# Five shared batches ahead of the experts instead of four, the first one's up steps moved into attention, expert weights loaded into their final place, and the loop over pairs written out

## The chip, the cores and the metric

The kernel runs on one core of a Trainium2 chip. The metric is the time of one execution on the device, in microseconds (us). A core has TensorE (PE, matrix products), VectorE (DVE), ScalarE (ACT) and GpSimd (POOL), a SyncE (SP) that issues DMAs, and 16 DMA engines; each engine runs its own instructions in order, and they wait for one another by semaphores.

## The reference, cut to what matters

One transformer layer in fp32 on x of 8 batches x 512 tokens x 256 values.

```python
x = x + attention(layernorm(x))        # 16 heads of 16, causal, W_Q, W_K, W_V, W_O 256x256
n = layernorm(x)
# FFN of n, 4096 tokens
shared = silu(n @ shared_w_gate.T) * (n @ shared_w_up.T) @ shared_w_down.T    # 704 hidden values
shared = shared * sigmoid(n @ shared_gate_w.T)
probs = softmax(n @ gate_w.T)          # 16 experts
rw, sel = top_k(probs, 2); rw = rw / rw.sum(-1)
for each token and each of its 2 experts e:
    g, u = split(n @ w_gate_up[e]); out += rw * ((silu(g) * u) @ w_down[e])   # 128 hidden values
x = x + out + shared
```

## The kernel before, in words

Products that have to be exact are made of three: each fp32 operand is split into a high part (rounded, by a copy on ACT) and a low part (what is left, by a subtraction on DVE), and `exact_product` issues hi x hi, hi x lo and lo x hi (lines 177, 178, 179 of the profile).

The program has two blocks one after the other, with a barrier of all engines between them.

**Block 1, `build_attention`.** Every engine walks one hand-written list of steps, `TURN`, once per batch, each entry with an offset of batch: S are scores and exps, max the row maxima, PV the product with V, oT/oTT transposes of its result, O the output projection, x2T and L the transposed xn2 and the router's logits, R the top 8, W the split of the shared weights. The eight PSUM banks are taken in the order of the steps (`Schedule`); a step waits until the step eight banks earlier has been emptied. The last turn (it = 8) has only what is left of batch 7. In its end DVE normalises x1 to xn2 itself (L580), SP stores xn2 (L371) and x1 (L376), and PE makes the last logits (L807).

**Block 2, `build_ffn`.** Four stages:
- *First half*, batches 0 to 3 (`FIRST = 4`) of the shared FFN. `shared` on PE: six up steps (12 products of 128x512 each, 6 in the last, which holds 64 gate and 64 up rows), the transposes of the next batch (L1423), then the down product (72 products of 128x256). ACT does silu (L1120) and the high part of h (L1125), DVE the product (L1299), the low part (L1302), and at the batch's end adds gate x result to x1 (L1317). Beside batch 0 DVE does the routing (L1220 to L1254: counts, prefix sums, slots), one part behind each step, then the weights (L1212 to L1216) and `experts_of_tiles` (L1259 to L1267). Once the slots are known, POOL scatters the 4096 rows of xn2 twice to the experts' rows in HBM (L1091, 64 indirect DMAs). Beside batches 1 to 3 the 16 experts' weights come one by one through two staging buffers (L1003) and are split (L1136, L1339).
- *Pairs*: 80 tiles of 128 rows, as 40 pairs, each tile of one expert: load (L1012), transpose x (L1480), gate and up, silu and product, transpose h (L1497), down, result (L1158), store (L1016). `fours_loop` runs four pairs per turn: the first and last four are written out, the 32 pairs between run in a hardware loop with a register. PE reads the experts' numbers from SBUF at the head and in the middle of a turn (`experts_of`).
- *Second half*, batches 4 to 7 of the shared FFN. Beside them POOL gathers each token's two rows (L1103, 64 indirect DMAs), and DVE adds them with their weights (L1323) to the stored results of the batches 0 to 6, some tiles behind each step (`TILES_BESIDE`).
- The last four tiles' rows and the last batch's result are added at the very end and stored in two parts.

SP's list holds the loads of xn2 and x1 for each batch, the rows for the scatter, the experts and the stores, in one order. x1 of a batch is loaded only when the stored result of the one before has left its buffer, and rows for the scatter when the rows two batches earlier are scattered.

Of the kernel before, what the change touches and what calls it, by code (L numbers as in the profile page):

```python
# [5 lines left out]
P = 128  # L6
B, S, D = 8, 512, 256
# [43 lines left out]
for g in range(GROUPS):  # L51
# [10 lines left out]
    ("max", 0, 1, 1), ("max", 0, 1, 2), ("oTT", -1, 0), ("oTT", -1, 1), ("K", 1, 1), ("max", 0, 1, 3), ("S", 0, 0, 0, 0),  # L62
# [12 lines left out]
def steps_of_turn(it):  # L75

    steps = []
    for kind, offset, *rest in TURN:
        if kind == "W":
# [10 lines left out]
EMPTIED_BY = {"xT": "dve", "Q": "dve", "K": "dve", "max": "dve", "mT": "act", "V": "act", "oT": "dve", "oTT": "dve",  # L90
              "O": "dve", "x2T": "act", "L": "dve"}
BANKS_OF = {"S": HALVES, "PV": 1}
SPLIT_STEPS = ("xT", "Q", "K", "oTT")


class Schedule:
# [29 lines left out]
    def freed(self, kind, which, n=0):  # L126

        if kind == "S":
            b, u, g, p = which
            return "exp", HALVES * (PAIRS * (GROUPS * (UNITS * b + u) + g) + p) + n + 1  # L130
        if kind == "PV":
            return "copy", UNITS * GROUPS * which[0] + which[1] + 1
# [1468 lines left out]
```

## Time and profile before

| | |
|---|---|
| three runs | 805.0, 805.0 and 809.97 us, median 805.0 |
| profiled execution | 800.1 us, its span 798.4 us |
| mean granted TensorE clock | 0.966 |
| busy in the span | PE 711.2 us (89%), DVE 524.7, ACT 401.5, POOL 326.8 |
| block 2 begins | 444.05 us |
| first pair's product | 570.62 us |
| second half's first product | 694.37 us |

The span is the time from the first to the last recorded work; 1.7 us lie around it. A busy PE is not PE at its peak. The granted clock of 1.00 is 2.4 GHz, 0.50 is 1.2 GHz.

### The profile page before, as it was taken

To read this page: it belongs to the slowest core of one execution; us is meant where nothing else is said; L and a number is where in the kernel's file an instruction comes from. 1 tells how busy PE (TensorE), PEld (TensorE's weight loads), DVE (VectorE), ACT (ScalarE), POOL (GpSimd) and SP (SyncE) were. 2 spreads that over 40 slices of the span, in tenths; PEclk is the share of its full clock that TensorE was granted. 3 is DMA by queue.
4 is the path that set the end of the run, shared out by engine and by line. 5 is a ranking of instruction groups with operands and counts; after the bars stand their busy time and mean duration, and the time that the engine had idled before them with its cause. 6 is when DMAs were issued, how large, how long until landed. Compare 5 with 4: busy or idle time off the path is not lost. (4 is left out here: it accounts for less than half of the span.)

```text
span 798.4 us, 17094 instructions
## 1 busy us (share of the span) xinstructions
PE 711.2 (89%) x5970; PEld 560.7 (70%) x5971; DVE 524.7 (66%) x1158; ACT 401.5 (50%) x777; POOL 326.8 (41%) x678
## 2 busy tenths in 40 slices
PE   1489999999999999999874879999699999999997
PEld 1456576676767667676643678887599989888886
DVE  6287787888878787887814494465445444466667
ACT  3116657565765656676671223344266565533232
POOL 5203536272552627354571127577100000077771
PEclk9889999999999999999998798999799999999999
DMA  5578667575876757577041218777554554478763
GB/s 158 204 244 292 212 240 260 175 258 185 290 265 206 261 193 241 189 264 232 21 155 35 98 53 282 264 236 259 171 186 154 186 169 151 133 229 279 242 211 115
DMA packets 102503, 159.72 MB, mean 200 GB/s; under 512 B 7712, under 2 KB 78368, under 8 KB 98208
## 3 DMA queue, kind: packets, MB, share of 16 engines
q1 hardware_dynamic: 96288, 141.99, 53.3%
q0 software_dynamic: 6144, 16.79, 6.3%
q8 instruction: 44, 0.72, 0.4%
q14 instruction: 27, 0.22, 0.1%
HBM read 86.66 MB, written 71.83 MB: 199 GB/s over the span
## 5 line engine op out<-in xcount | busy, mean ns | idle before, releaser
L615 DVE TENSOR_REDUCE neg_max<-ps_w 128x1 f32<-128x512 f32 (+3 forms) x352 | 202.5, 632 | 43.5 <-PE ps_w L720 43.5
L552 ACT ACTIVATE probs<-ps_w 128x512 f32<-128x512 f32 x320 | 165.2, 617 | 9.9 <-PE ps_w L736 9.8
L401 POOL TENSOR_TENSOR pool_scratch<-minus_half 1x1 f32<-1x1 f32 x190 | 35.0, 184 | 237.0 <-ACT probs L552 201.1
L1103 POOL DMA_INDIRECT ex<-yg_dram,slots x64 | 65.1, 1017 | 153.9 <-DMA yg_dram<-y 134.7
L433 POOL TENSOR_SCALAR_AFFINE_SELECT probs<-probs 128x256 f32<-128x256 f32 (+1 forms) x224 | 94.1, 431 | 0.0
L1091 POOL DMA_INDIRECT xg_dram<-srow,slots x64 | 65.5, 1023 | 51.8 <-DVE slots L1254 26.6
L177 PE MATMUL ps_f<-stacks 128*128 128x512 f32 x176 | 72.7, 413 | 9.6 <-DVE xT_lo_f L1272 6.8
L1120 ACT ACTIVATE silu<-ps_f 128x512 f32<-128x512 f32 (+1 forms) x48 | 28.5, 594 | 103.7 <-PE ps_f L179 103.7
L747 PE MATMUL ps_w<-probs,v_aug 128*32 128x512 f32 (+3 forms) x1024 | 77.1, 442 | 3.8 <-POOL probs L433 3.8
L178 PE MATMUL ps_f<-xT_lo_f,stacks 128*128 128x512 f32 x176 | 70.8, 403 | 0.0
L179 PE MATMUL ps_f<-stacks 128*128 128x512 f32 x176 | 70.8, 402 | 0.0
L1299 DVE TENSOR_TENSOR h<-ps_f,silu 128x512 f32<-128x512 f32 (+1 forms) x48 | 33.1, 690 | 46.7 <-ACT silu L1120 44.7
L747 PEld LDWEIGHTS ps_w<-probs,v_aug 128*32 128x32 f32 x1024 | 30.8, 111 | 44.7 <-issue 34.2
L560 ACT ACTIVATE o_raw<-ps_w 128x512 f32<-128x512 f32 x32 | 19.4, 606 | 76.3 <-PE ps_w L747 76.3
L177 PE MATMUL ps_f<-stacks,h_hi 128*128 128x256 f32 (+1 forms) x192 | 55.0, 286 | 1.8 <-DVE h_lo L1302 1.8
L177 PE MATMUL ps_f<-ex,stacks 128*128 x160 | 48.4, 302 | 5.8 <-issue 4.3
L179 PE MATMUL ps_f<-stacks,h_lo 128*128 128x256 f32 (+1 forms) x192 | 53.4, 278 | 0.0
L178 PE MATMUL ps_f<-w_lo,h_hi 128*128 128x256 f32 (+1 forms) x192 | 53.4, 278 | 0.0
L720 PE MATMUL ps_w<-mask_rows,ident_rows 64*128 64x128 bf16 (+2 forms) x704 | 53.2, 229 | 0.0
L712 PE MATMUL ps_w<-stacks 64*128 64x256 f32 (+3 forms) x256 | 41.4, 376 | 10.8 <-DMA stacks<-qk_dram 10.2
L1353 DVE TENSOR_TENSOR h<-ps_f,silu 128x256 f32<-128x256 f32 x40 | 17.0, 424 | 48.6 <-ACT silu L1148 48.6
L177 PEld LDWEIGHTS ps_f<-stacks 128*128 128x128 f32 x176 | 34.1, 194 | 20.1 <-DVE xT_lo_f L1272 6.4
(170 smaller groups left out, 1792.5 us busy)
## 6 DMA issues: line engine op xcount, KB each, us to landing
qk_dram<-projected SPq DMA_DIRECT2D x96, 256.0 KB, 5.6
stacks<-qk_dram SPq DMA_DIRECT2D x16, 1024.0 KB, 7.3
xg_dram<-zeros SPq DMA_DIRECT2D x20, 512.0 KB, 10.3
srow<-xg_dram SPq DMA_DIRECT2D x40, 256.0 KB, 2.8
q_st<-qk_dram SPq DMA_DIRECT2D x8, 1024.0 KB, 5.0
k_st<-qk_dram SPq DMA_DIRECT2D x8, 1024.0 KB, 8.3
projected<-experts SPq DMA_DIRECT2D x16, 384.0 KB, 4.9
yg_dram<-projected SPq DMA_DIRECT2D x20, 256.0 KB, 2.2
```

The lines of the kernel that those rows point to most:

```text
L177: pe.matmul(out, s_hi, m_hi, start=start, stop=False)
L178: pe.matmul(out, s_hi, m_lo, start=False, stop=False)
L179: return pe.matmul(out, s_lo, m_hi, start=False, stop=stop)
L401: ticks = Ticks(pool, pool_ticks, lambda: pool.tensor_tensor(out=pool_scratch[:, 0:1], in0=minus_half[0:1, 0:1], in1=minus_half[0:1, 0:1], ...
L433: masked = pool.affine_select(out=diagonal, in_=diagonal, compare_op=ALU.is_ge, fill=0.0, base=0, pattern=[[0, number], [1, P]], channel_m ...
L552: act.activation(probs[:, g, p * PAIR + half * BANK:p * PAIR + (half + 1) * BANK], ps_w[:, plan.bank(kind, which, half), :], ACT.Exp).then ...
L615: dve.tensor_reduce(out=neg_max[u][:, qt, first:first + len(heads)], in_=bank[:, 0:len(heads) * width].rearrange("p (h n) -> p h n", h=len ...
L712: pe.matmul(outs[half][:, i * width:(i + 1) * width], q_st[u][b % 2][rows, slot, qt * P:(qt + 1) * P], k_st[u][b % 2][rows, slot, 0:width] ...
L720: made = pe.matmul(blocks, ident_rows[rows, part, :], mask_rows[rows, part, first:P].unsqueeze(1).to_broadcast([ROWS, len(heads), P - first]),
L747: made = pe.matmul(out[hh * STRIP:(hh + 1) * STRIP, kt * P:S], v_aug[b % 2][:, kt, group * GH + hh, :], probs[:, g, pair * PAIR + col:pair ...
L1091: pool.indirect_dma_start(out=xg_rows, out_offset=bass.IndirectOffsetOnAxis(ap=slots[:, c, n:n + 1], axis=0), in_=srow[:, b % 2, t, :], in ...
L1103: pool.indirect_dma_start(out=back[:, m, c, :], out_offset=None, in_=yg_rows, in_offset=bass.IndirectOffsetOnAxis(ap=slots[:, c, m:m + 1], ...
```

## The change

1. `FIRST = 5`: batches 0 to 4 of the shared FFN run ahead of the experts, 5 to 7 behind them. `EXPERTS_FROM` gives four experts to split to each of the batches 1 to 4; `TILES_BESIDE` spreads the 28 tiles over three batches.
2. Batch 0's transposes (`fT`) and up steps (`U` 0 to 6; step j also splits h of j-1) are steps of attention's last turn. Their operands and results get memory that both blocks share. In block 2, batch 0 has its down product alone; its result is added by DVE behind the second step of batch 1. Batch 1's transposes come first in block 2, and SP loads its xn2 at the end of block 1.
3. DVE does the whole routing in one go in batch 0's place, `experts_of_tiles` behind the third step of batch 1. The ranks go to banks 4 and 5.
4. The experts' weights come in four loads of four experts, straight to where their low parts will stand; ACT makes the high part from there and DVE the low part in place. The loads are issued at the start of block 2.
5. The rows for the scatter are loaded beside batches 1 to 3 (`SCATTERED_BESIDE`).
6. The loop over pairs becomes one slot per pair, written out 41 times, on all four engines; the experts' numbers are read at each even pair.

```diff
 TURN = [
...
+    ("S", -1, 1, 1, 1), ("fT", 8, 0), ("fT", 8, 1), ("max", 0, 0, 6), ("R", -2), ("S", -1, 1, 1, 2),
...
+    ("S", -1, 1, 1, 4), ("PV", -1, 2), ("U", 8, 0),
...
+    ("PV", -1, 3), ("oT", -1, 2), ("mT", 0, 0), ("oT", -1, 3), ("U", 8, 1),
...
+    ("oTT", -1, 0), ("oTT", -1, 1), ("U", 8, 2),
...
+    ("O", -1, 1), ("moments_x1", -1), ("U", 8, 3), ("U", 8, 4),
...
+    ("x2T", -1, 0), ("x2T", -1, 1), ("U", 8, 5),
...
+    ("L", -1, 1), ("U", 8, 6),
...
 ]
...
         sp.wait_ge(first_in, 16)
+        sp.wait_ge(work_ready, plan.upto("ready", "fT", DK - 1))
+        sp.dma_start(xn_f, xn2_v[1]).then_inc(first_in, 16)
+        sp.wait_ge(first_in, 32)
...
@@ ACT, a step of block 1 @@
+            elif kind == "fT":
+                act.activation(xf_hi[:, which, :], bank, ACT.Copy).then_inc(hi_done, 1)
+            elif kind == "U":
+                if which < FT:
+                    act.wait_ge(up_made, which + 1)
+                    if which >= 2:
+                        act.wait_ge(h_made, which - 1)
+                    act.activation(silu[0:filled(which), which % 2, :], ps_w[0:filled(which), plan.bank(kind, which), :], ACT.Silu).then_inc(silu_made, 1)
+                if which > 0:
+                    act.wait_ge(h_made, which)
+                    part = filled(which - 1)
+                    act.activation(h_hi[0:part, which - 1, :], h[0:part, (which - 1) % 2, :], ACT.Copy).then_inc(h_hi_made, 1)
...
@@ PE, a step of block 1 @@
+        def shared_up(j):
+            if j == 0:
+                pe.wait_ge(freed["dve"], plan.freed("fT", DK - 1)[1])
+                pe.wait_ge(shared_lo, 4)
+            for i in range(banks_of("U", j)):
+                out, col = bank_for("U", j, i), (2 * j + i) * P
+                for k in range(DK):
+                    at = slice(k * 2 * FF + col, k * 2 * FF + col + P)
+                    made = exact_product(pe, out, (up_parts[0][:, at], up_parts[1][:, at]), (xf_hi[:, k, :], xT_lo[:, k, :]),
+                                         start=k == 0, stop=k == DK - 1)
+            made.then_inc(up_made, 1)
...
-FIRST = 4
+FIRST = 5
-EXPERTS_FROM = [0, 0, 5, 10, 16]
-TILES_BESIDE = {4: (0, 1, 1, 1, 1, 1, 2), 5: (1, 1, 1, 1, 1, 1, 1), 6: (1, 1, 1, 1, 1, 1, 1), 7: (1, 1, 1, 1, 1, 1, 1)}
+EXPERTS_FROM = [0, 0, 4, 8, 12, 16]
+LOADS = 4
+PER_LOAD = E // LOADS
+TILES_BESIDE = {5: (0, 1, 1, 2, 1, 2, 1), 6: (1, 2, 1, 2, 1, 2, 1), 7: (1, 2, 1, 2, 1, 2, 1)}
+SCATTERED_BESIDE = {0: (), 1: (2, 3, 4), 2: (5, 6), 3: (7,), 4: ()}
...
@@ SP, block 2 @@
             load_x1(b)
-            for e in range(EXPERTS_FROM[b], EXPERTS_FROM[b + 1]):
-                if e >= 2:
-                    sp.wait_ge(w_split, e - 1)
-                sp.dma_start(stage[:, e % 2, :], experts[e]).then_inc(stage_in[e % 2], 16)
-                if e % 2 and e // 2 < B - 2:
-                    rows_of(e // 2 + 2)
+            for ahead in SCATTERED_BESIDE[b]:
+                rows_of(ahead)
             sp.wait_ge(y_done, TB * (b + 1))
...
         for b in range(2):
             rows_of(b)
+        for n in range(LOADS):
+            some = slice(n * PER_LOAD, (n + 1) * PER_LOAD)
+            sp.dma_start(ex[:, some, 1, :].bitcast(f32), experts[some].rearrange("e p n -> p e n")).then_inc(experts_in[n], 16)
...
@@ DVE, block 2 @@
         def shared(b, more, beside):
+            if b == 0:
+                for j in range(FT + 1):
+                    routing(j)
+                weights()
+                return
             for j in range(FT + 1):
...
                 if j >= 1:
                     beside(j - 1)
-                if b == 0:
-                    routing(j)
-            if b == 0:
-                weights()
-                experts_of_tiles()
+                if b == 1 and j == 1:
+                    add_shared(0)
+                if b == 1 and j == 2:
+                    experts_of_tiles()
...
@@ PE, block 2 @@
         def shared(b, more):
+            if b:
+                up(b)
+            if b and more:
+                transpose_xn(b + 1)
+            down(b)
...
+        def slot(n):
+            if is_pair(n - 1):
+                transpose_h(n - 1)
+            if n >= 0:
+                transpose_x(n + 2) if is_pair(n + 2) else transpose_xn(FIRST, [n + 2 - TILE_PAIRS]) if n + 2 < TILE_PAIRS + DK else None
+            if is_pair(n + 1):
+                gate_and_up(n + 1)
+            if is_pair(n - 1):
+                project_down(n - 1)
...
+        def start(b):
+            transpose_xn(b + 1)
+            ranks()
...
+        for n in range(-1, TILE_PAIRS + 1):
+            slot(n)
```

## Rows read from the trace of the kernel before

**Rows 1.** Busy time by window, the stage ahead of the experts; the last figure is GB/s
```profile
444.00:564.00 120.00, 107.14 (x586) 90.72 (x586) 73.48 (x126) 44.51 (x74) 66.85 (x70) 0.94 0.60 202
```
**Rows 2.** The chain that ended last, where the pairs begin: start, us, what
```profile
564.35 3.42 DMA srow<-xg_dram
...
570.62 0.57 PE ps_f L177
```
**Rows 3.** The source line of the scatters
```profile
L1091 POOL DMA_INDIRECT xg_dram<-srow,slots x64: 957/963/1614, 472.2 to 561.8; - x64
```
**Rows 4.** Timeline of DVE, routing beside batch 0
```profile
453.24 0.68 DVE L1220 COPY projected<-ps_f 128x512 f32<-128x512 f32 x1
...
471.67 0.20 DVE L1254 CAST slots<-projected 128x64 int32<-128x64 f32 x1
...
472.87 0.82 DVE L1259 TENSOR_TENSOR y<-projected 128x640 f32<-128x640 f32 x1
...
477.51 1.29 DVE L1272 TENSOR_TENSOR xT_lo_f<-ps_f,stacks 128x512 fp32r<-128x512 f32 x2
```
**Rows 5.** The chain, two batches of the second half: their transposes
```profile
709.91 0.88 PE ps_f L1423 x8
...
734.94 0.87 PE ps_f L1423 x8
```
**Rows 6.** The source line of the gathers; the second row is of its last nine
```profile
L1103 POOL DMA_INDIRECT ex<-yg_dram,slots x64: 945/949/1395, 697.5 to 780.8; - x64
...
DMA to landing us min/median/max: 2.7/3.5/5.5
```
**Rows 7.** Timeline of PE, one turn of the loop over pairs
```profile
633.04 0.38 PE L177 MATMUL ps_f<-ex,stacks 128*128 x1 [0.60 <-issue]
...
641.99 0.44 PE L1497 MATMUL ps_f<-ident,h 128*128 128x128 f32 x2
...
644.43 0.28 PE L179 MATMUL ps_f<-ex,h_lo 128*128 x1
645.33 0.38 PE L177 MATMUL ps_f<-ex,stacks 128*128 x1 [0.62 <-issue]
```
**Rows 8.** Timeline of PE, attention's tail; in brackets the idle time before
```profile
418.47 2.36 PE L747 MATMUL ps_w<-probs,v_aug 128*32 128x512 f32 x32 [1.98 <-POOL probs L433]
...
423.07 1.09 PE L683 MATMUL ps_w<-ident,o_tok 128*128 128x128 f32 x8 [0.81 <-DVE o_tok L624]
425.74 0.39 PE L177 MATMUL ps_w<-w_hi,oT_hi 128*128 128x256 f32 x1 [1.57 <-DVE oT_lo L595]
...
436.12 1.97 PE L683 MATMUL ps_w<-ident,xn 128*128 128x128 f32 x8 [7.25 <-DVE xn L580]
```
**Rows 9.** Timeline of PE, first up products of batch 1
```profile
478.86 0.79 PE L177 MATMUL ps_f<-stacks 128*128 128x512 f32 x1 [4.41 <-DVE xT_lo_f L1272]
...
484.57 0.52 PE L178 MATMUL ps_f<-xT_lo_f,stacks 128*128 128x512 f32 x1
484.92 0.39 PE L179 MATMUL ps_f<-stacks 128*128 128x512 f32 x1
485.15 0.40 PE L177 MATMUL ps_f<-stacks 128*128 128x512 f32 x1
```
**Rows 10.** Timeline of ACT, the last exps
```profile
407.58 9.90 ACT L552 ACTIVATE probs<-ps_w 128x512 f32<-128x512 f32 x20
```
**Rows 11.** DMA issues from 426 to 450: KB each, us to landing
```profile
srow<-xn_dram SPq DMA_DIRECT2D x2, 512.0 KB, 4.3
...
x_dram<-x SPq DMA_DIRECT2D x1, 512.0 KB, 5.5
```
**Rows 12.** Busy time by window, behind the border: granted clock, DMA share, GB/s at the end
```profile
446.00:447.00 1.00, 0.03 (x1) 0.00 (x0) 0.84 (x2) 0.91 (x2) 0.00 (x0) 0.50 1.06 372
```
**Rows 13.** Timelines of PE and DVE, where the second half begins and ends
```profile
694.37 0.47 PE L177 MATMUL ps_f<-stacks 128*128 128x512 f32 x1 [0.97 <-DVE xT_lo_f L1272]
...
794.08 1.66 DVE L1317 SCALAR_TENSOR_TENSOR projected<-ps_f,gate,projected 128x256 f32<-128x256 f32 x4
```

More of the change, by code:

```diff
@@ L104, in __init__ @@
         assert len(self.place) == len(self.steps)
-        self.banked = [(*step, n) for step in self.steps for n in range(BANKS_OF.get(step[0], step[0] in EMPTIED_BY))]
+        self.banked = [(*step, n) for step in self.steps for n in range(banks_of(*step))]
         self.banked_place = {step: n for n, step in enumerate(self.banked)}
@@ L763, in step @@
                 transposed(kind, which, xn)
+            elif kind == "fT":
+                out = bank_for(kind, which)
+                pe.wait_ge(first_in, 16)
+                for t in range(TB):
+                    made = pe.transpose(out[:, t * P:(t + 1) * P], xn_f[:, t, which * P:(which + 1) * P], ident[:, :])
+                made.then_inc(work_ready, 1)
+            elif kind == "U":
+                if which < FT:
+                    shared_up(which)
             elif kind in ("Q", "K"):
@@ L863, in ffn_views, with shared_views, filled, build_ffn @@
             rows.rearrange("p (t d) -> p t d", t=TB), others.rearrange("p (t d) -> p t d", t=TB))
-def build_ffn(nc, ctx, stacks, projected, w_lo, logits_all, top, index, slots, experts_of_four, weight, gate, x1_dram, xn2_dram, xg_dram, yg_dram, y1_dram,
+def shared_views(stacks, rows_held, heads_held):
+    xT_hi = stacks[:, 2 * UP_COLS + DOWN_COLS:2 * UP_COLS + DOWN_COLS + DK * S].rearrange("p (k t) -> p k t", k=DK)
+    silu, h = (rows_held[:, n].rearrange("p (two t) -> p two t", two=2) for n in range(2))
+    h_hi, h_lo = (heads_held[:, n * FT * S:(n + 1) * FT * S].rearrange("p (j t) -> p j t", j=FT) for n in range(2))
+    return xT_hi, silu, h, h_hi, h_lo
+def filled(j):
+    return P if j < FT - 1 else FF_LAST
+def build_ffn(nc, ctx, stacks, projected, w_lo, x_lower, rows_held, heads_held, logits_all, top, index, slots, experts_of_four, weight, gate, x1_dram, xn2_dram, xg_dram, yg_dram, y1_dram,
               ident, experts, out):
@@ L1178, in tiles @@
         def tiles():
             act.wait_ge(x1_left, 16 * FIRST)
[L1180 to L1186 removed]
+            for q in range(2):
+                split_x(q)
+            slots_of_loop(slot)
+        def start(b):
+            act.wait_ge(args_ready, 2)
+            act.activation(exps[:, :, :], args[:, :, :], ACT.Exp).then_inc(exps_ready, 1)
+            split_xT(b + 1)
@@ L1188, in _ @@
+        two_halves(start, first_half, tiles, shared)
     @block.vector
@@ L1313, in shared @@
             beside(FT)
-            dve.wait_ge(x1_in, 16 * (b + 1))
-            for t in range(TB):
-                dve.wait_ge(down_ready, b * 2 + (t // 2 + 1))
-                dve.scalar_tensor_tensor(out=x1[:, t, :], in0=ps[:, 6 + t // 2, (t % 2) * D:(t % 2 + 1) * D],
-                                         scalar=gate[:, bass.ds(b * TB + t, 1)], in1=x1[:, t, :], op0=ALU.mult, op1=ALU.add).then_inc(y_done, 1)
+            add_shared(b)
         def add_rows(c, m, done):
@@ L1444, in shared, with down @@
                 last.then_inc(up_ready, 1)
-                if b == 0 and j == 0:
-                    ranks()
-            if b == 0:
-                pe.wait_ge(counts_left, 1)
-                pe.wait_ge(routing_steps, RANK_READ)
-            if more:
-                transpose_xn(b + 1)
+        def down(b):
             pe.wait_ge(y_done, b * TB)
```

341 lines of the change are left out of this document (164 added, 177 removed), and 19 rows, old and new, of the table TURN.

## Prediction

> **What bounds the kernel now.** I cut the span by stage (busy time by window, then the timelines) and asked in each what ends last, since TensorE (PE) is at nine tenths or more almost everywhere and the page's totals don't tell. Attention lasts to 444.05, the four shared batches ahead of the experts to 561.7, the 40 pairs from 570.62 to 693.2, the four batches behind them to 794, and the stores to 798.4. Ahead of the experts PE is busy for 107 of 120 us [rows 1], and the chain of waits shows that it isn't what ends last: behind the last of 64 scatters on GpSimd (POOL) come its landing, a load, a transpose and a split [rows 2]. The scatters run from 472.2, when the slots are known, to 561.8 [rows 3, 4]. Four batches want 100 us of PE there (25.0 each, by the undisturbed ones [rows 5]) and get 117. Behind the experts it is PE: 694.37 + 4 x 25 = 794, while the 64 gathers start their last at 780.8 [rows 6]. The pairs run at 12.29 us per four, with an idle of 0.6 at the loop's head [rows 7]. In attention's tail PE is free for much of the time, but a single chain (exp, mask, P V, transposes, output projection, norm) runs through it, and PE is one of its links [rows 8].
>
> I write A for the start of the second block (444.05 before) and set up its new value first.
>
> **Attention's tail.** It gains two transposes of xn2 and 66 products of 512 columns, 0.23 us apart [rows 9]: 15.3 us of PE, with six silus and eight copies on ScalarE (ACT) and 14 operations on VectorE (DVE).
> - The two copies of the transposes stand among 20 exps, which run without a gap at 9.90/20 = 0.50 each [rows 10]: 1.0 on the chain.
> - U(8,0), 12 products or 2.8 us, stands between the last two P V. The last one was at 418.47 [rows 8]; now the one ahead of it ends at 417.5, U(8,0) at 420.3: 1.8 later with the exps' 1.0.
> - U(8,1) stands between the o transposes and those of o_tok. PE was idle there for 0.81 to 1.0 [rows 8]: 1.8 more.
> - U(8,2) fills the 1.57 idle ahead of the output projection [rows 8] and pushes it by 1.2; its operations and those of U(8,1) are queued on DVE around the lowering of oT, 0.1 more. The last x1, its norm and xn2 come at 436.06 + 4.9 = 440.9.
> - U(8,3) and U(8,4), 5.6 us, fit into PE's 7.25 idle [rows 8] and cost nothing; U(8,5), U(8,6) and the logits end before what follows. If that cover were short, every us would go onto the chain.
> - The load of silu's table falls into ACT's wait for U(8,0).
> - SP now loads xn2 of batch 1 inside this block, behind its waits for both stores. The x1 store, SP's second issue behind xn2 (0.4 later), lands 5.5 after it [rows 11], so 5.9 behind xn2; issue and landing of the new load are 0.4 + 4.3 [rows 11], the barrier 0.2. The block ends 10.8 behind xn2, where it was 8.0.
> A is 440.9 + 10.8 = 451.7: **7.7 later**. For the bounds: 4 if the fills fit better, 11 if the product steps queue up on DVE.
>
> **Ahead of the experts.** Batch 0 has only its down product left, five batches in place of four.
> - DVE does the choices first; the ranks can run at A+3.6, so the down product of batch 0 starts at A+4.9. PE is again at 0.50 of its clock (1.2 GHz) after the idle at the border, as behind the border before [rows 12]; 8.9 (25.0 less 15.3 and the 0.9 of the transposes [rows 5]) and some 1.1 for the clock: A+14.9.
> - Routing no longer alternates with batch 0's steps. Its operations from places to slots add up to 9.8 (18 of them, before spread over 453.24 to 471.87 [rows 4]); from A+5.2 the slots are ready at A+15.0, before at A+27.8. Even with the 89.6 that the scatters took with their waits [rows 3], the rows are complete at A+108. This was the bound and is none now.
> - Batch 1's steps queue on DVE behind routing. Its second step is followed by the add of batch 0's result, which waits for x1. That load is issued at A+15.1, behind two row loads and four expert loads, 7.3 MB in all. At the 372 GB/s of a busy stretch [rows 12], and 260 once the scatters' 100 (128 KB per 1.27 us) go beside it, it lands at A+26; unhindered, with the 4.3 of [rows 11], at A+20. I take 26: the x1 store in the tail, issued behind a single other one, already took 5.5 and not 4.3 [rows 11]. Then come the adds, one step, and experts_of_tiles, 4.65 us [rows 4], ahead of the next step. PE waits twice, 2.0 and 4.1 us. The second is as long as the 4.4 before 478.86, behind which the products were 0.43 apart up to 484.57, and 0.23 from 484.92 [rows 9]: 5.7 us at half clock, or 2.9 lost. Batch 1 costs 25.0 + 9.0 (bounds 4 and 13): A+48.9.
> - Two batches of 25.05 and one of 24.15 (no transposes behind it) end at A+123.2. The experts' split from their final place removes 16 loads of 384 KB and the waits for the staging buffers; what is left, a copy on ACT and a subtraction on DVE for each expert, four of them in a batch's 25 us, hides under PE; without that cover it would be near 1 us each on DVE.
> - Then SP has the store of the last y1 (1.2 + 0.4) ahead of the first pair's load, and from the issue of that load to the first pair's product it takes 6.3 [rows 2], with 0.6 more for the store in the queue: 8.5. First product at **A+131.7**; before at A+126.6. That is 5.1 later.
>
> The Trainium skill (DMA: Bandwidth & Descriptors, "Queues, rings and completion order") states that each DMA engine consumes the descriptors of one ring in order, and takes turns between rings at packet boundaries. By it x1 comes behind the experts as I set it; at A+20 the batch would cost 2.2 less. No row of before shows the order, since no load stood behind that much.
>
> **The pairs.** The order written out is: transpose h, transpose x, gate and up, down. At the old loop's head the first product starts 0.90 behind the last one, where 0.12 is usual, and two transposes of h come 0.17 late in the body: 12.29 less 0.78 and 0.17 is 11.34 per four [rows 7]. Over nine heads that gives 8.6. At the end nothing stands between the last transposes of h and the down products: two waits for a copy and a subtraction, by an estimate 0.8 each, 1.6 given back. **7 less**; 9 if those waits are covered, nothing if each of the 20 reads of the experts' numbers costs 0.4, out of the 0.6 that the head shows.
>
> **Behind the experts.** Three batches end 75 us behind the pairs, so PE no longer ends last. The gathers keep their pace, 83.3 from first to last start, and start 4.3 behind the last pair, whose products end just ahead of 693.4 [rows 6, 13]. The last lands 3.2 on (landings are 2.7 to 5.5 [rows 6]); one first add and four second ones (2.1), 1.7 for the adds of the last batch and 2.7 for its store [rows 13] follow: 697.5 + 83.3 + 3.2 + 2.1 + 0.1 + 1.7 + 2.7 = 790.6 on the old scale, against 798.4: **7.7 less** with rounding. A whole batch of 25 us less gives only this, because the gathers come next. Bounds 6 and 8.5.
>
> **The sum.** 7.7 + 5.1 - 7 - 7.7 = -1.9. The profiled execution had a span of 798.4 in a time of 800.1, 1.7 around it, which stays: 798.2. The median of the runs shown is 805.0, 4.9 above the profiled one; the same difference taken from it gives **803.1**. The 15 us of up steps are not removed from PE, and the batch that they belong to is moved from a stage where PE was the bound to one where it was not, but becomes it.
>
> **Rivals.** (1) *The clock stays up and the slots run dry of waits.* The waits of 2.0 and 4.1 come from estimates. Were the second shorter, and the clock stayed up, 2.9 and the 1.1 of batch 0's down part go, and the pairs give 9 and not 7: 803.1 - 6 = **797**. For it: the new up steps keep PE at work closer to the border; against it: behind idles of 4.4 and 7.25 the clock was at 0.50 [rows 8, 9, 12]. (2) *The written-out pairs give nothing*: the head's 0.6 is the number read and not the branch. For it: the releaser is "issue" and nothing else is seen there; against it: the same read stands in the middle of the body, where no idle shows. 803.1 + 7 = **810**. (3) *The expert loads are slow* (the other side). They are 6.3 MB in four issues with x1 behind them, and batch 0's add blocks DVE, and so batch 1's steps and PE. At 372 GB/s it costs 2; the mean of the stage is 202 [rows 1]. At that, 7.3 MB are there at A+38, x1 at A+41, 15 us later: 803.1 + 15 = **818**. It turns the sign at a mean of about 310 GB/s and gives over 1% slower under about 235. Against it: three loads in a row ran at 372 [rows 12]. (4) *The tail isn't filled but pushed*, each of the first five product steps with its whole 2.8 on the chain: 4 more, **807**.
>
> **How the numbers follow.** Forecast 0.48 (its own range 799 to 808), (1) 0.22, (2) 0.11, (3) 0.10, (4) 0.09. One per cent (8 us) is about what a measurement of this kernel can tell from no change, since its three runs differ by 5. Faster by more than that: (1) with most of its chance and the low end of the forecast, 0.24. Slower: (3) and a share of (2), 0.13. Within it: 0.63. The range of 794 to 812 leaves out the greater part of (3) and a corner of (1) and (2).
>
> **What would show it.** Right: second block at about 452; first scatter some 15 us behind it; PE idle for 2 and 4 us in batch 1's up steps, with the clock at 0.50 behind them; no idle of POOL that PE waits for ahead of the experts, and PE the last there; 11.3 per four pairs; DVE waiting for gathers in the last 20 us. Wrong: x1 landed well before batch 1's second product; gaps of 0.3 and more at each second pair; PE, not the gathers, last at the end.

## The result, and the profile after

| | before | after |
|---|---|---|
| median, first comparison | 805.44 us (805.0 to 809.97, 4 runs) | 796.01 us (794.73 to 797.4, 4 runs) |
| profiled execution, its span | 800.1, 798.4 us | 796.59, 794.8 us |
| median, timed again in a later comparison | 803.63 us (11 runs) | 795.66 us (6 runs) |

The ratio to the kernel before is 0.9868, 95% interval 0.9833 to 0.9902, and when timed again 0.9902 (0.9879 to 0.9925). The kernel is about 1% faster, 8 to 9 us. The forecast was 803, inside a range of 794 to 812. The time lies in the range, but 7 us under the forecast and outside the likeliest case's own range of 799 to 808.

The rows below are of the changed kernel. First busy time by window, ahead of the experts, in the columns of [rows 1]:
```profile
452.00:573.00 121.00, 113.88 (x658) 100.30 (x658) 75.08 (x128) 45.71 (x75) 68.85 (x70) 0.95 0.60 209
```
PE idles for 7 us in a stretch where it idled for 13 [rows 1]: it has become the last. The chain that ended last (start, us, what) says the same. What leads to the first pair is the last result of the fifth batch and its store, and not a step of POOL as in the chain of [rows 2]:
```profile
572.47 1.67 DVE projected L1366 x4
574.15 0.36 SPq L1080
574.61 3.60 DMA srow<-xg_dram
...
581.06 0.58 PE ps_f L186
```
The source line of the scatters, against [rows 3]: they begin 4.7 us earlier, counted from the start of the execution, although the second block begins 8.4 later, and the last one begins 27 us ahead of the first pair's product.
```profile
L1165 POOL DMA_INDIRECT xg_dram<-srow,slots x64: 957/963/1691, 467.5 to 554.3; - x64
```
The timeline of DVE: the slots are ready 14.5 us behind the start of the block at 452.48 (before 27.6 [rows 4]), and batch 0's result waits for x1 (idle time and releaser in brackets).
```profile
466.99 0.20 DVE L1325 CAST slots<-projected 128x64 int32<-128x64 f32 x1
...
477.50 1.66 DVE L1366 SCALAR_TENSOR_TENSOR projected<-ps_f,gate,projected 128x256 f32<-128x256 f32 x4 [1.56 <-DMA projected<-x_dram]
```
The timeline of PE, in three places: the tail of attention [rows 8], the two waits in batch 1's up steps [rows 9], and the pairs [rows 7].
```profile
415.67 4.05 PE L789 MATMUL ps_w<-probs,v_aug 128*32 128x512 f32 x32 [0.62 <-DVE x_lower L621]
...
422.60 2.36 PE L789 MATMUL ps_w<-probs,v_aug 128*32 128x512 f32 x32
...
442.94 1.09 PE L725 MATMUL ps_w<-ident,xn 128*128 128x128 f32 x8 [1.81 <-DVE xn L606]
...
452.48 1.94 PE L1491 MATMUL ps_f<-ident,projected 128*128 128x128 f32 x8 [5.34 <-PEq L1632]
...
479.81 0.50 PE L186 MATMUL ps_f<-stacks 128*128 128x512 f32 x1 [1.32 <-DVE rows_held L1383]
...
486.34 0.50 PE L186 MATMUL ps_f<-stacks 128*128 128x512 f32 x1 [3.51 <-DVE rows_held L1383]
...
601.43 0.36 PE L186 MATMUL ps_f<-ex,stacks 128*128 x1
...
604.23 0.36 PE L186 MATMUL ps_f<-ex,stacks 128*128 x1
...
694.92 0.38 PE L186 MATMUL ps_f<-ex,heads_held 128*128 x1 [0.85 <-DVE heads_held L1437]
...
697.41 0.38 PE L186 MATMUL ps_f<-ex,heads_held 128*128 x1 [1.29 <-DVE heads_held L1437]
```
The 7.25 us in which PE waited for xn [rows 8] are down to 1.81: the up steps found idle time to fill there. From pair to pair it is 2.80 us without a gap, 11.2 per four, where the loop took 12.29 [rows 7]. Busy time by window, the third figure from the end of a row being the granted clock:
```profile
450.00:460.00 10.00, 5.71 (x24) 5.00 (x25) 6.34 (x12) 3.89 (x5) 1.50 (x7) 0.50 0.76 259
480.00:490.00 10.00, 6.49 (x27) 5.18 (x27) 9.70 (x18) 4.23 (x7) 6.76 (x7) 0.87 0.93 306
490.00:500.00 10.00, 10.00 (x76) 9.60 (x75) 4.43 (x9) 1.59 (x3) 7.84 (x8) 0.96 0.44 149
775.00:795.00 20.00, 4.54 (x37) 4.21 (x35) 8.95 (x20) 0.00 (x0) 9.04 (x9) 0.65 0.46 144
```
The last row shows PE at work for 4.54 of the last 20 us: behind the pairs it has become the gathers that end last. Their source line, against [rows 6], and the last adds on DVE, against [rows 13]:
```profile
L1177 POOL DMA_INDIRECT ex<-yg_dram,slots x64: 942/949/1457, 702.5 to 785.6; - x64
...
DMA to landing us min/median/max: 2.7/3.9/7.1
```
```profile
788.42 2.07 DVE L1402 SCALAR_TENSOR_TENSOR projected<-ex,weight,projected 128x256 f32<-128x256 f32 x5 [2.06 <-DMA ex<-yg_dram,slots]
790.53 1.66 DVE L1366 SCALAR_TENSOR_TENSOR projected<-ps_f,gate,projected 128x256 f32<-128x256 f32 x4
```

### The profile page after: what moved, and what is told of

Same layout as the page of the kernel before. It is cut to its first block and busy times, and to the rows that moved or that the text cites. A ratio compares the mean times of both kernels' runs of the same rounds, so it can differ in the third digit from the quotient of the medians.

```text
span 794.8 us, 16690 instructions
## 1 busy us (share of the span) xinstructions
PE 708.8 (89%) x5970; PEld 563.3 (71%) x5970; DVE 528.6 (67%) x1158; ACT 400.6 (50%) x779; POOL 328.1 (41%) x678
## 5 line engine op out<-in xcount | busy, mean ns | idle before, releaser
L1165 POOL DMA_INDIRECT xg_dram<-srow,slots x64 | 67.4, 1053 | 33.9 <-issue 18.9
L1196 ACT ACTIVATE rows_held<-ps_f 128x512 f32<-128x512 f32 (+1 forms) x42 | 25.0, 596 | 108.8 <-PE ps_f L188 108.8
L789 PE MATMUL ps_w<-probs,v_aug 128*32 128x512 f32 (+3 forms) x1024 | 78.9, 451 | 0.9 <-DVE x_lower L621 0.6
L186 PE MATMUL ps_f<-stacks 128*128 128x512 f32 x154 | 62.0, 403 | 9.4 <-DVE rows_held L1383 5.1
L188 PE MATMUL ps_f<-stacks 128*128 128x512 f32 x154 | 61.2, 398 | 0.0
L187 PE MATMUL ps_f<-x_lower,stacks 128*128 128x512 f32 x154 | 61.1, 397 | 0.0
L1383 DVE TENSOR_TENSOR rows_held<-ps_f,rows_held 128x512 f32<-128x512 f32 (+1 forms) x42 | 29.0, 691 | 43.1 <-ACT rows_held L1196 42.8
L186 PE MATMUL ps_f<-stacks,heads_held 128*128 128x256 f32 (+1 forms) x192 | 56.8, 296 | 0.0
L187 PE MATMUL ps_f<-w_lo,heads_held 128*128 128x256 f32 (+1 forms) x192 | 55.0, 287 | 0.0
L188 PE MATMUL ps_f<-stacks,heads_held 128*128 128x256 f32 (+1 forms) x192 | 54.8, 286 | 0.0
L186 PE MATMUL ps_f<-ex,stacks 128*128 x160 | 49.3, 308 | 0.8 <-DVE x_lower L1425 0.8
L187 PE MATMUL ps_f<-ex,stacks 128*128 x160 | 45.9, 287 | 0.0
L188 PE MATMUL ps_f<-ex,x_lower 128*128 x160 | 45.8, 287 | 0.0
## 6 DMA issues: line engine op xcount, KB each, us to landing
ex<-experts SPq DMA_DIRECT2D x4, 1536.0 KB, 14.7
```

The costliest lines, as they stand in the source:

```text
L186: pe.matmul(out, s_hi, m_hi, start=start, stop=False)
L187: pe.matmul(out, s_hi, m_lo, start=False, stop=False)
L188: return pe.matmul(out, s_lo, m_hi, start=False, stop=stop)
L789: made = pe.matmul(out[hh * STRIP:(hh + 1) * STRIP, kt * P:S], v_aug[b % 2][:, kt, group * GH + hh, :], probs[:, g, pair * PAIR + col:pair ...
L1165: pool.indirect_dma_start(out=xg_rows, out_offset=bass.IndirectOffsetOnAxis(ap=slots[:, c, n:n + 1], axis=0), in_=srow[:, b % 2, t, :], in ...
```

## Experiments

Twelve runs were made in three comparisons, each beside the kernel before. In all of them the same four points were read: A, the start of the second block (its first transposes), the first transposes of the pairs, the first gather, and the end of the span. What lies between them adds up to the span, but for rounding, in us:

| profiled execution | A | A to pairs | pairs to gather | gather to end | span |
|---|---|---|---|---|---|
| before | 444.1 | 123.8 | 129.6 | 100.9 | 798.4 |
| before_again | 445.0 | 125.0 | 131.1 | 101.6 | 802.7 |
| before_slots | 445.9 | 124.1 | 122.2 | 100.2 | 792.4 |
| before_first5 | 444.35 | 148.3 | 131.0 | 91.2 | 814.8 |
| after | 452.5 | 125.9 | 124.1 | 92.3 | 794.8 |
| after_again | 454.35 | 124.3 | 123.5 | 91.7 | 793.8 |
| after_tiles_early | 450.6 | 121.6 | 123.3 | 91.2 | 786.7 |
| after_x1_ahead | 452.4 | 125.9 | 124.3 | 92.2 | 794.8 |
| after_xn_early | 452.3 | 126.2 | 123.7 | 91.3 | 793.5 |
| five_tiles_xn | 450.5 | 121.3 | 124.3 | 91.9 | 788.0 |
| after_first4 | 453.3 | 108.4 | 123.1 | 101.4 | 786.1 |
| best2 | 450.4 | 108.7 | 124.0 | 101.3 | 784.4 |
| best3 | 450.55 | 110.8 | 124.2 | 100.9 | 786.5 |
| best4 | 450.3 | 106.8 | 124.4 | 101.6 | 783.1 |

A moves by up to 4 us between executions with the same block 1 (450.6 to 454.35 with the up steps in the tail), and has moved before the tail begins: its last P V but one, the one of 4.05 us above, starts at 413.83 in after_tiles_early and at 417.51 in after_again. The granted clock of the first 100 us (0.90 to 0.93) doesn't order them. Yet, counted from A, the stretches of one design repeat within 1.6 us. One profile against one profile (800.1 and 796.59) shows 3.5 us where the medians of the first comparison show 9.4.

**before_again** is the kernel before, with no edit.

> The kernel before, unchanged, against itself. Ratio 1.000 (0.996 to 1.004). Theory: its profiled execution of 800.1 us was an outlier 5 us under its other runs, and a new profile has a span near 803 to 804, with the 5 us more spread over attention (block 2 would begin at 446 or later instead of 444.05) or as idle of PE. Rival: the spans are always near 798 and the runs of 805 to 810 have their extra time outside of what the profile shows; then the new profile has 444.0, 570.6 and 694.4 again and a span of 798 to 799.

Measured: 804.36 us, ratio 1.0034 (1.0006 to 1.0062), so a third of one per cent is what two identical kernels can differ by here, and an interval below may be off by as much. The span was 802.7 and not 798. Of its 4.3 us more, 0.9 are ahead of the border, 1.2 ahead of the pairs, 1.5 at their end, where the last store's landing took 3.96 us, and 0.7 behind the first gather. Theory right on the outlier, wrong on the place: it is a little of each. The timelines of PE, where the last P V stands in the tail:
```profile
417.82 3.58 PE L747 MATMUL ps_w<-probs,v_aug 128*32 128x512 f32 x32 [1.97 <-POOL probs L433]
...
445.03 1.94 PE L1423 MATMUL ps_f<-ident,projected 128*128 128x128 f32 x8 [1.71 <-PEq L1561]
```
The same 32 products that took 2.36 in [rows 8] take 3.58, with the granted clock at 0.70 and then 0.50.

**before_slots**, the kernel before with only the pairs written out (the diff cut to the loop; the order of steps in a slot is that of the change, point 6):
```diff
-        with engine.Fori(FOUR, TILE_PAIRS - 2 * FOUR + 1, FOUR) as q:
-            four_pairs(q, True)
+        for n in range(-1, TILE_PAIRS + 1):
+            slot(n)
```


> The kernel before with only the pairs written out. Theory: each head of the old loop cost some 0.6 to 0.8 us, nine heads; after the change the stretch from the first pair's product to the first gather went from 126.9 to 121.4 us, so this alone gives 5.5 us less: ratio 0.993 of the kernel before, 11.2 us per four pairs. Rival (2) of the prediction, the written-out pairs give nothing and the stretch got shorter by the other layout of weights: ratio 1.000.

Measured: 794.31 us, ratio 0.9899 (0.9855 to 0.9943), 8 us less where the theory said 5.5. The timeline of PE, from one pair to the next, and the source line of the gathers:
```profile
600.34 0.36 PE L177 MATMUL ps_f<-ex,stacks 128*128 x1
...
603.13 0.36 PE L177 MATMUL ps_f<-ex,stacks 128*128 x1
```
```profile
L1102 POOL DMA_INDIRECT ex<-yg_dram,slots x64: 942/946/1370, 692.2 to 775.2; - x64
```
2.79 us per pair, as in the changed kernel. From the pairs' first transposes to the first gather it takes 122.2 where the three executions with the loop took 129.6 to 131.1, 8.4 less than their mean. This edit alone has the full size of the whole change. Rival (2) is out: the gain came without the new layout of weights. The edit took away the loop and also changed the order of the steps within a pair; no run tells these two apart.

**before_first5**, the kernel before with only the fifth batch ahead:
```diff
-FIRST = 4
-EXPERTS_FROM = [0, 0, 5, 10, 16]
-TILES_BESIDE = {4: (0, 1, 1, 1, 1, 1, 2), 5: (1, 1, 1, 1, 1, 1, 1), 6: (1, 1, 1, 1, 1, 1, 1), 7: (1, 1, 1, 1, 1, 1, 1)}
+FIRST = 5
+EXPERTS_FROM = [0, 0, 4, 8, 12, 16]
+TILES_BESIDE = {5: (0, 1, 1, 2, 1, 2, 1), 6: (1, 2, 1, 2, 1, 2, 1), 7: (1, 2, 1, 2, 1, 2, 1)}
```


> The kernel before with only the fifth batch ahead of the experts (its up steps not in attention's tail). Theory: that stage's scatters are hidden by 5 batches and it becomes bound by PE: 5 x 25 us plus the stops of batch 0, first pair's product at about 590 to 596 us instead of 570.6 (+19 to +25), and behind the experts the gathers give back 8: +11 to +17 us, ratio 1.014 to 1.021. Rival: the stage was bound by scatters and landing so much that most of a batch fits into it: first product at 578, ratio 1.000.

Measured: 817.11 us, ratio 1.0198 (1.0166 to 1.0229). The timeline of PE at the pairs:
```profile
592.64 1.94 PE L1480 MATMUL ps_f<-ident,srow 128*128 128x128 f32 x8 [5.29 <-DMA srow<-xg_dram]
```
Ahead 148.3 where it was 123.8 to 125.0, behind 91.2 where it was 100.9: 24 us more and 10 less. Nearly the whole batch of 25 us is paid ahead, and less than half of it comes back. The same row of the kernel before says why:
```profile
567.90 1.94 PE L1480 MATMUL ps_f<-ident,srow 128*128 128x128 f32 x8 [6.24 <-DMA srow<-xg_dram]
```
Here the last scatter starts at 569.1, far ahead of the pairs, and PE still idles for 5.29 us: the last result has to be added and stored, and the first rows loaded. Of the 6.24 us in the kernel before, only 1 was thus due to the scatters. They did end last there, but PE stood right behind them.

**after_first4** is the changed kernel with the three tables of four batches, the diff above read backwards.

> The changed kernel with four batches ahead and four behind. Theory: ahead of the experts it loses a batch of 25 us of PE, but then the scatters end last again (slots at A+14.5, scatters to A+102, then landing, load, transpose, 8.8): first pair's product at about 563.5 instead of 581.1, -17.5; behind the experts PE is last again, +8.6. So 9 us less than the changed kernel, ratio to the kernel before 0.976. Rival: moving the batch is what made the changed kernel faster, and four ahead give the time of before's border and end again: 8 us more than the changed kernel, ratio 0.997.

Measured: 786.13 us, ratio 0.98 (0.9772 to 0.9828), where the theory said 0.976, just outside the interval, and the rival 0.997. The timeline of PE, and the source line of the scatters:
```profile
561.65 1.94 PE L1554 MATMUL ps_f<-ident,srow 128*128 128x128 f32 x8 [14.19 <-DMA srow<-xg_dram]
```
```profile
L1165 POOL DMA_INDIRECT xg_dram<-srow,slots x64: 956/962/1896, 468.3 to 556.4; - x64
```
Now PE idles for 14.19 us and the last scatter is 5.3 us ahead of the pairs. Of the 14.19 us, 5.3 are the idle that PE has there anyway, so it has 8.9 to spare and a batch of 25 should cost 16. Ahead it takes 108.4 where five batches took 125.9 and 124.3, behind 101.4 where they took 92.3 and 91.7: 16.7 less and 9.4 more. The fifth batch ahead is thus the one part of the change that is shown to cost time: 7.7 and 8.7 us by the spans, 5.5 and 8.2 by the two ratios of the changed kernel. The theory's 9 less is at the upper end of this.

**after_tiles_early**, the changed kernel with the tiles' experts in batch 0's place:
```diff
                 weights()
+                experts_of_tiles()
                 return
...
-                if b == 1 and j == 2:
-                    experts_of_tiles()
```


> The changed kernel with the tiles' experts worked out by DVE in batch 0's place, right behind the weights, where it waits for x1 anyway, instead of behind batch 1's third step. Theory: PE's wait of 3.51 us in batch 1 (486.34) goes, and most of what the clock lost behind it (granted 0.87 in 480 to 490), some 1.5 us; ahead of the experts PE is the bound, so first pair's product comes 4 to 5 us earlier and so does the end: ratio to the kernel before 0.981 if the changed kernel is at 0.987. Rival: DVE starts x1's add later, the first wait grows by as much as the second shrinks, and PE has no gain: 0.987.

Measured: 791.6 us, ratio 0.9839 (0.9813 to 0.9866). The timeline of DVE, where the add of batch 0 still waits for x1, and busy time by window:
```profile
475.68 1.66 DVE L1366 SCALAR_TENSOR_TENSOR projected<-ps_f,gate,projected 128x256 f32<-128x256 f32 x4 [1.50 <-DMA projected<-x_dram]
```
```profile
480.00:490.00 10.00, 9.18 (x68) 8.44 (x67) 6.97 (x11) 4.44 (x8) 7.67 (x8) 1.00 0.81 256
```
The wait for x1 is as long as before, 1.50 against 1.56, and starts as far behind A (25.1 against 25.0), so that the 4.65 us of the tiles' experts lay in time that DVE had. PE is busy for 9.18 of 10 us where it was 6.49 (9.18 too from 478.1 to 488.1, as far behind A as the changed kernel's row), and the clock stays at 1.00. Two waits are left in the batch, 0.66, and 0.82 for the next xn2. From A to the pairs it takes 121.6, against 125.9, 124.3 and 125.9: 3.8 less, of the 4 to 5 expected. The times alone wouldn't settle it: the ratio lies between the theory's 0.981 and the rival's 0.987, both just outside its interval; five_tiles_xn below has it beside the changed kernel.

**after_x1_ahead**, the changed kernel with x1 ahead of three of the expert loads (the first expert load stays at the block's start):
```diff
             load_x1(b)
+            if b == 0:
+                for n in range(1, LOADS):
+                    load_experts(n)
...
-        for n in range(LOADS):
-            some = slice(n * PER_LOAD, (n + 1) * PER_LOAD)
-            sp.dma_start(ex[:, some, 1, :].bitcast(f32), experts[some].rearrange("e p n -> p e n")).then_inc(experts_in[n], 16)
+        load_experts(0)
```


> The changed kernel with x1 of batch 0 loaded ahead of three of the four expert loads. Theory: x1 lands at about A+17 to A+20 instead of A+25.1 (A is the start of the second block), batch 0's result is added as soon as DVE comes to it, the wait of 1.32 us goes and the second one of 3.51 begins earlier and stays: 1.3 to 2 us less, ratio 0.985. Rival (3) of the prediction in its small form: the transfers of the experts are what PE waits for, so both waits go: 5 us less, 0.981. Third: x1's place is given away to the experts' loads that are then late for batch 1's split on ACT and DVE: 0.987 or more.

Measured: 796.96 us, ratio 0.9913 (0.9883 to 0.9943), no gain, where the theory said 0.985. SP's issues, the timeline of PE, and the chain of waits:
```profile
467.14 0.36 SPq L1060 DMA_DIRECT2D projected<-x_dram  x1
467.55 1.75 SPq L1069 DMA_DIRECT2D ex<-experts  x3
```
```profile
484.92 0.79 PE L186 MATMUL ps_f<-stacks 128*128 128x512 f32 x1 [3.53 <-DVE rows_held L1388]
...
489.35 1.10 PE L1496 MATMUL ps_f<-ident,projected 128*128 128x128 f32 x8 [1.51 <-DMA projected<-xn_dram]
```
```profile
478.12 11.18 DMA projected<-xn_dram
```
x1 lands in 3.8 us where it took 10.3. The wait of 1.32 is gone and the next one comes 1.42 earlier, as the theory said. But x1 is issued at 467.14 here and at 467.21 in the changed kernel, in both 0.2 behind the slots; the expert loads, that had used the time until then, now run from 467.55 on and stand in front of the next xn2, which lands after 11.18 us where it took about 4. PE waits 1.51 for it. The third theory is right in kind, with another victim than it named.

**after_xn_early**, the changed kernel with the load of batch 1's xn2 issued ahead of the store of the last xn2 and x1:
```diff
+            if it == B:
+                sp.wait_ge(first_in, 16)
+                sp.wait_ge(work_ready, plan.upto("ready", "fT", DK - 1))
+                sp.dma_start(xn_f, xn2_v[1]).then_inc(first_in, 16)
             if before:
                 sp.wait_ge(xn2_done, it)
                 sp.dma_start(xn2_v[it - 1], xn2[:, :, :]).then_inc(xn2_out, 16)
...
-        sp.dma_start(xn_f, xn2_v[1]).then_inc(first_in, 16)
```


> The changed kernel with xn2 of batch 1 loaded ahead of the two stores that end the first block, instead of behind them. Theory: its issue and landing are the last thing in that block: the barrier opened 1.4 to 3 us behind what the stores alone need. Block 2 begins at A = 449.5 to 450 instead of 452.5 and everything behind it comes as much earlier: ratio 0.983 to 0.984. Rival: the x1 store's landing, 5.5 us, is what the barrier waits for: A stays within 0.5 us, ratio 0.987.

Measured: 795.22 us, ratio 0.9874 (0.9847 to 0.9902). SP's issues around the border, of this kernel and then of the changed one:
```profile
444.79 0.38 SPq L386 DMA_DIRECT2D xn_dram<-xn  x1
445.21 0.51 SPq L391 DMA_DIRECT2D x_dram<-x  x1
452.26 0.93 SPq L1071 DMA_DIRECT2D srow<-xn_dram  x2
```
```profile
442.92 0.38 SPq L382 DMA_DIRECT2D xn_dram<-xn  x1
...
448.14 0.36 SPq L409 DMA_DIRECT2D projected<-xn_dram  x1
452.44 0.92 SPq L1070 DMA_DIRECT2D srow<-xn_dram  x2
453.40 6.06 SPq L1140 DMA_DIRECT2D ex<-experts  x4
```
From the store of xn2 to the border it is 7.5 us where it was 9.5: 2.05 less, of the 2.5 to 3 expected. What holds the border now is in the timeline of POOL, whose last part of the shared weights' split ends at 451.94, 0.34 us ahead of the border, while x1's store has landed by 450.0:
```profile
450.14 1.80 POOL L503 TENSOR_TENSOR w_lo<-projected,stacks 128x768 fp32r<-128x768 f32 x1 [6.50 <-ACT stacks L591]
```
A itself stood still, because attention's tail came 2 us later in this execution. The ratio is the rival's 0.987 and not the theory's 0.983 to 0.984, so by the time alone there is no gain to be told.

**best3** has four batches ahead and all three small edits.

> Four batches ahead and all three small edits (tiles' experts early, x1 ahead of three expert loads, xn2's load ahead of the stores). Theory: with four batches the scatters are the bound ahead of the experts, so the two edits that shorten PE's waits are worth nothing there, and only the earlier border counts, since the slots come as much earlier: 3 us less than four batches alone (0.980), ratio 0.976. Rival: the three gains add up, 9 us: ratio 0.969.

Measured: 788.78 us, ratio 0.9803 (0.9776 to 0.983): neither the theory's 0.976 nor the rival's 0.969. A came 2.7 us earlier than with four batches alone and the pairs only 0.3. In the chain of waits:
```profile
475.45 10.90 DMA y_dram<-projected
486.36 0.36 SPq L1061
486.76 6.15 DMA srow<-xn_dram
```
The store of batch 0 took 10.90 us behind the expert loads, the rows for the scatter are behind it in SP's order, and POOL waited 6.0 us for them. x1 ahead of the expert loads cost nothing with five batches; with four it delays the scatters, and these end last there.

**after_again** is the changed kernel, with no edit.

> The changed kernel, unchanged, timed again beside the kernel before and the variants of this call. Theory: ratio to the kernel before 0.9868 as at first, within 0.984 to 0.990; between profiled executions the start of the second block moves by up to 2 us with the clock of attention's first 100 us, and stretches counted from that start don't: first gather 250 us behind it, end 92 us behind the first gather. Rival: the first comparison was off by its four runs, and the ratio is 0.991 or more, as the variant with x1 ahead had.

Measured: 795.66 us, ratio 0.9902 (0.9879 to 0.9925), just over the edge of what was expected. A to gather 247.8 and gather to end 91.7, the first of them 2.2 under what was expected. The granted clock of the first 100 us isn't what moves A, as said under the table. The change is worth 0.8 to 1.7%.

**five_tiles_xn** is the changed kernel with both of the edits that gave something.

> Five batches ahead, with the tiles' experts early and xn2's load of batch 1 ahead of the last two stores of the first block. Theory: the two act at different places of one chain on which PE is the bound, so they add up: 5 us for the first (its profile shows 245 us from the border to the first gather instead of 250), 2 for the second (7.5 us from xn2's store to the border instead of 9.5): ratio 0.978. Rival: the first alone measured 0.984 and the second alone 0.987, so the sum is 0.984.

Measured: 789.71 us, ratio 0.9823 (0.9797 to 0.9848), 6 us less than the changed kernel in the same comparison. Its A to pairs is 121.3, and A is 450.5 with the same start of the tail as the changed kernel had at 452.5: by the stretches the two add up, 2 for the border and 3.8 in batch 1. The theory's ratio of 0.978 lies outside the interval all the same and the rival's 0.984 inside: the theory had reckoned 5 and 2 us from a changed kernel at 0.987, and it is at 0.9902 in this comparison.

**best2** has four batches ahead and the early load of xn2.

> Four batches ahead and xn2's load of batch 1 ahead of the stores. Theory: the slots, and with them the scatters that are the bound there, come 2 us earlier: 2 us less than four batches alone (ratio 0.980), 0.9775. Rival: the scatters' pace depends on what else is on the DMA engines, and takes the 2 us back: 0.980.

Measured: 784.7 us, ratio 0.9749 (0.9717 to 0.9781), with the rival's 0.980 outside. The border came the 2 us earlier (with some of A's own movement), and the stretch to the pairs stayed, 108.7 for 108.4: the slots are the head of the chain there, and the scatters' pace didn't take it back (88.3 us from first to last start, against 88.1).

**best4** has in addition the tiles' experts early.

> Four batches ahead, xn2's load ahead of the stores, tiles' experts early; x1 stays behind the expert loads. Theory: with four batches PE has some 14 us to spare ahead of the experts, so the early tiles' experts, worth 5 us with five batches, are worth nothing: the same as without them, 0.9775. Rival: they are worth their 5 us here too: 0.972.

Measured: 784.31 us, ratio 0.975 (0.9727 to 0.9774), between the theory's 0.9775 and the rival's 0.972, both just outside; best2 in the same comparison has 0.9749. One of its six executions took 1677.42 us and is left out of the ratio; I don't know why it did. The timeline of PE:
```profile
557.07 1.94 PE L1554 MATMUL ps_f<-ident,srow 128*128 128x128 f32 x8 [15.47 <-DMA srow<-xg_dram]
```
PE waits 15.47 us for the scatters whatever it is spared before: the early tiles' experts, worth 3.8 us with five batches, are worth nothing in the time with four: the medians of best2 and best4 differ by 0.4. Its stretch ahead of the pairs is 1.9 shorter in the profile, from scatters that ran at a better pace (86.5 us against 88.3). Why they did isn't known. Against five_tiles_xn, which differs from it in the fifth batch alone and ran beside it, best4 is 5.4 us faster. best2 and best4 are the fastest measured: 2.5% under the kernel before and 1.4% under the changed one (784.5 to 795.66).

## Why the prediction was right, and where it was off

The forecast's sum was made against one profile. For the measured size of its four terms I take means over the executions of the same design in the table: A over four kernels with the old tail and five with the new one (without those with xn2 early), the other stretches over two or three, which spread by up to 1.6 us.

| term | forecast | before, mean | after, mean | measured |
|---|---|---|---|---|
| border A | +7.7 | 444.85 | 452.6 | +7.8 |
| A to pairs | +5.1 | 124.3 | 125.1 | +0.8 |
| pairs to first gather | -7 | 130.6 | 123.8 | -6.8 |
| first gather to end | -7.7 | 100.9 | 92.0 | -8.9 |
| sum | -1.9 | 800.6 | 793.5 | -7.1 |

- **The tail** was right in place, and in sum partly by luck. Its fills fit under the 7.25 us. xn was ready at 442.9 (predicted 440.9), mostly since 32 products of P V took 4.05 us and not 2.36, with the granted clock at 0.50 (below). The border behind xn2 took 9.5 and not 10.8, so that two errors of 2.0 and 1.3 nearly cancel. Rival (4) didn't come: the 2.0 are the clock's, not product steps on the chain. Its price doesn't follow from its own words either: five steps with their whole 2.8 are 14 us, of which the forecast has 4, so some 10 more and not 4.
- **Ahead of the experts** is the term that was mis-sized: +0.8 for +5.1. By the changed kernel's own profile the first product came at A+128.6 and not A+131.7, 3.1 less. Batch 0's down part ran from A+4.2 to A+14.8 (predicted A+4.9 to A+14.9; 8.9 there is 8.8 by its own numbers): its start was 0.7 early, but the clock stayed at 0.50 until 460, which lost 1.7 and not 1.1. Batch 1 took 31.9 and not 34.0. This is the estimate that was furthest off: its two waits were 1.32 and 3.51 (predicted 2.0 and 4.1), and behind the second the clock lost 1.7 us (0.13 and 0.04 of two windows of ten) where the prediction had 2.9. The other three batches took 73.9 for 74.3, and from PE's last product to the pairs it was 8.0 for 8.5. 0.1 + 2.1 + 0.4 + 0.5 = 3.1. The remaining 1.2 of the 4.3 is the spread of single profiles: before's mean is 0.5 above its first profile, after's 0.8 below. Rival (1) is nearest in time (797), but not in its mechanism: its second wait of less than 4.1 came, the clock that stays up didn't, and the pairs gave 6.8 and not 9.
- **What bounded that stage before** was read too far. The scatters did end last, but before_first5 shows PE within 1 us of them, so the batch wasn't moved to where PE had room. The stage stayed nearly as long because batch 1 starts 20.0 us nearer to A (A+14.8, where it was A+34.8), 15 of them the up steps that went to the tail.
- **What the prediction said of x1 was right**: issued at A+14.7 (A+15.1), batch 0's add at A+25.0 (A+26). The Trainium skill's page DMA: Bandwidth & Descriptors, "Queues, rings and completion order", by which one ring's descriptors are consumed in order, agrees with the two orders tried: x1 takes 10.3 us to land behind four expert loads and 3.8 ahead of three of them, and xn2 takes 11.18 us when the three expert loads are ahead of it. Rival (3), slow expert loads, didn't come: from 460 to 470 the DMA engines moved 402 GB/s.
- **The pairs**: -6.8, and -8.4 with this edit alone. From the first to the last transposes it takes 109.9 in the changed kernel and 108.3 in before_slots, where it took 117.8: 7.9 and 9.5 less. The end gave back 2.5 and 2.1, with waits of 0.85 and 1.29. Forecast: 8.6 and 1.6. Reading the experts' numbers at each even pair costs nothing that shows.
- **Behind the experts**: -8.9 for -7.7, by the mechanism named: PE at work for 4.54 of the last 20 us, and DVE waiting for gathers up to 788.42. before_first5 has it alone, -9.7.
- **The level.** The forecast's sum was put on a median of 805.0; later comparisons had 802.4, 803.9 and 803.6. Of the 9.4 us between the first medians 1.5 to 3 are this. The 4.9 us between before's profile and its median, which the forecast carried over as a constant, were a step that failed too: the changed kernel's profiled execution lies among its other runs. So of the 7.1 us between 803.1 and 796.0, 5.2 are the four terms and 1.9 the level.

So the prediction said rightly that PE becomes the bound ahead of the experts and the gathers behind them, and what the tail, the pairs and the end cost or give; it took the stage ahead of the experts 4 us too dear. It priced the six parts as one and so didn't see that one of them alone has the whole gain and that the fifth batch takes some away. Parts alone: the pairs written out, -8; the fifth batch in the new design, +17 ahead and -9 behind; routing in one go with the up steps in the tail, and the weights in place, what is left, -8.2 by the medians and -6.3 by the profiles (after_first4 against before_slots: the border 7.4 later, the first scatter 13.3 nearer to it, from there to the pairs 2.4 less, 2.0 given back behind). The parts that make up this last figure weren't tried apart.

What stays open: why the stretch from pairs to gather is 1 to 2 us longer in the kernels with the new layout (123.1 to 124.4) than in before_slots (122.2), and why A moves by 4 us. And where PE ends last ahead of the pairs, it idles for 5.3 us: the last scatter of the changed kernel starts at 554.3, yet SP issues the first pair's load only at 574.61, since the store of the fifth batch's result stands ahead of it in its list. No run moved that load.

## What to carry to other kernels

A batch of work that is moved to another stage costs its whole size where the engine ends last and only what goes beyond its spare time where another ends last: here 17 us of 25 ahead, with 9 to spare, and 9 of 25 given back behind. Each stage's second bound is worth as much reading as its first, since a chain shows who ended last and not by how little. When several edits come together, price each by what ends last *in that stage with the others in*: early tiles' experts were worth 3.8 us under a bound by PE and nothing under a bound by scatters. A load put ahead in one queue puts another behind it; name who that is before counting the gain. And read a comparison of two single profiles by stretches, from a common event on, not by their ends.

## What the runs showed of the hardware that I had not expected

- TensorE's granted clock fell to 0.50 in attention's tail, with waits of only 0.42 to 0.62 us each ahead of it and the clock at 1.00 from 412 to 414. The 32 products of P V that follow, the last P V but one, took 3.75 to 4.05 us in all ten executions profiled with the up steps in the tail, and not the 2.36 of full clock; the last P V took 2.36 in all ten. Without these steps it is the other way round: the last but one took 2.36 in all four executions, and the last, behind a wait of 1.97 to 1.98 us, took 2.36, 2.36, 3.58 and 4.05. So the clock fell in two of these four executions, and 2.36 and 3.58 are of one and the same kernel, before and before_again. By window, in the changed kernel:
```profile
412.00:414.00 2.00, 1.10 (x10) 0.65 (x8) 0.00 (x0) 2.00 (x5) 1.70 (x6) 1.00 1.08 397
414.00:416.00 2.00, 0.89 (x11) 0.51 (x12) 1.08 (x2) 2.00 (x5) 0.58 (x3) 0.94 0.64 240
416.00:418.00 2.00, 2.00 (x13) 0.43 (x9) 1.20 (x13) 2.00 (x5) 1.47 (x6) 0.50 0.00 0
```
  What PE had done before the fall was 1.10 and 0.89 of 2 us.
- SP took 6.06 us to issue four loads of 1.5 MB behind two of 0.5 MB, and 1.75 for three of them behind one of 0.5 MB (after_x1_ahead). In the changed kernel nothing else was due on SP until 467.
